# Keys' and values' weights and the context as pairs of float16 in a fused attention and expert kernel

## The chip, the core and the metric

The kernel runs on one core of a Trainium2 chip. A core has five engines that run side by side, each through its own list of instructions in order: TensorE (PE, the matmuls; its weight loads are shown as PEld), VectorE (DVE), ScalarE (ACT), GpSimd (POOL) and SyncE (SP, which here only starts DMA transfers). An engine waits for another by a counter, a semaphore. The metric is the device time of one execution in microseconds (us), lower is better.

## The reference

Eight batches of 512 tokens with 256 channels go through a gated cross attention on a context of 512 rows with 128 channels, and then through eight experts of which each token takes two:

```python
x = x + tanh(g_xattn) * (softmax((LN(x) @ Wq) @ (ctx @ Wk).T / 8) @ (ctx @ Wv) @ Wo + bo)   # 16 heads of 64
probs = softmax(LN(x) @ gate_w.T); comb = the two largest of probs, per token
x = x + tanh(g_ffn) * sum_e comb[e] * (LN(x) @ expert_w[e].T + expert_b[e])
```

All data are float32. The products are made from high and low parts, so that they are nearly as exact as float32: an operand is rounded to a short type (the high part), the remainder is kept as a second one (the low part), and three matmuls, high with high, high with low and low with high, add up in one PSUM bank.

## The kernel before

**Jobs.** A batch is cut into 32 units: 8 pairs of heads times 4 tiles of 128 queries. Per unit PE makes the scores of two heads (`scores`, six matmuls into the bank pair `ST`), DVE takes the row maximum (`nmax`) and the `shifts` from it, ACT the exponential (`exp`, into `pf`) and then its float16 high part (`copy`, into `p_s`), POOL the low part (`low`), SP transposes both by DMA into `pt_s`, and six units later PE multiplies them with the values (`values`, into `PV`). Between units PE makes the other products, called jobs, into three shared banks `MB`: `q`, `k`, `v` (queries, keys, values), `xt`, `ot`, `x2t` (transposes), `wo`, `router`, `pair`, `gates`, `bias` and `bound`. ACT takes a job's high part (`take_hi`), DVE its low part or its sum (`take`); then the bank is free.

**Order.** What each engine does in which of the 32 rows is written out by hand in the tables PE_ORDER, ACT_ORDER, DVE_ORDER and POOL_ORDER, one for the first batch (FIRST), one for the next six (LOOP) and one for the last (LAST). Ahead of FIRST stands a prologue with the jobs `xt0, xt1, bound, k0, q0` of NEXT_JOBS (in LOOP these are jobs for the next batch); behind LAST stand the experts of the last batch (EPI). FIRST also prepares the output's and the experts' weights, which no other batch does.

**What the change touches.** A `k` job is three matmuls of 128x512 of `wk_s` and `kv_s` (L1364), a `v` job three of `kv_s` and `wv_s` (L1368). These three tiles have the type float32r, a float32 form that PE takes in one pass. The high parts are plain copies on ACT (L730, L764, L769; L779 in the loop), the low parts plain subtractions on POOL (L671, L686, L688, L691). `wk` and `wv` land in `pt_s`, which is not used yet, so that SP holds back the second transpose until the low parts are made (L575).

**The bound.** Every batch the row maxima of the context (`kmax`) are multiplied with those of the weights (`kv_w_max`) by PE in the job `bound`. DVE makes of it `v_div`, `v_mul`, `o_mul` and `s_val` (L918 to L973), POOL the scales `k_mul` and `q_out` (`scales`), with which the high and low parts of `k`, `q` and `v` are scaled into float16. In FIRST the job stands in row 21 of PE's table, and DVE takes it in row 22. ACT makes the next batch's context high part (`context`) in row 20, after the exponential of unit 20 and before that of unit 21; in LOOP `bound` stands in row 12 and `context` in row 24.

**Weights of the queries.** `wq` is already handled as a scaled float16 pair: DVE finds the largest weight (`wq_max`), PE sums it over the partitions (`summed`), DVE makes `q_mul` from it, and ACT and DVE make the two parts, the first 256 columns (`early`) in the prologue and the `rest` in FIRST.

Of the kernel before, what the change touches and what calls it, by code (L numbers as in the profile page):

```python
# [218 lines left out]
NEXT_JOBS = [("xt", 0), ("xt", 1), ("bound",), ("k", 0), ("q", 0), ("q", 1), ("k", 1)]  # L219
# [115 lines left out]
def build(nc, x, kv_t, g_xattn, g_ffn, wq, wk, wv, wo, bo, gate_t, expert_t, expert_b, out):  # L335
# [5 lines left out]
    with ctx:  # L341
# [14 lines left out]
        wk_s = sb("wk_s", [P, 2, INNER], F32R)  # L356
        wv_s = sb("wv_s", [P, 2, INNER], F32R)
# [13 lines left out]
        ones = sb("ones", [P, 1])  # L371
        kv_w_max = sb("kv_w_max", [P, 2])
# [17 lines left out]
        kv_s = sb("kv_s", [P, 2, TOKENS], F32R)  # L390
# [47 lines left out]
        stage_q = sb("stage_q", [P, LC, INNER])  # L438
        stage_o = sb("stage_o", [P, PAIRS, DIM])
# [18 lines left out]
        w_hi, wq_lo, wq_rest_lo, w_lo = sem("w_hi"), sem("wq_lo"), sem("wq_rest_lo"), sem("w_lo")  # L458
        late_step, late_hi, late_lo = sem("late_step"), sem("late_hi"), sem("late_lo")
# [52 lines left out]
        CONST_POOL = EXPERTS + 11  # L512
# [17 lines left out]
        def _(sp):  # L530
# [5 lines left out]
            sp.dma_start(stage_k, wk).then_inc(wk_in, 16)  # L536
            sp.dma_start(stage_v, wv).then_inc(wv_in, 16)
# [65 lines left out]
        def _(pool):  # L603
# [81 lines left out]
            pool.wait_ge(kv_hi, 1)  # L685
            pool.tensor_tensor(kv_s[:, 1, :], kvin[:, :], kv_s[:, 0, :].bitcast(F32), ALU.subtract).then_inc(kv_lo, 1)  # L686
            pool.wait_ge(w_hi, 1)
            pool.tensor_tensor(wk_s[:, 1, :], stage_k, wk_s[:, 0, :].bitcast(F32), ALU.subtract).then_inc(w_lo, 1)  # L688
            scales(0)
            pool.wait_ge(w_hi, 3)  # L690
            pool.tensor_tensor(wv_s[:, 1, :], stage_v, wv_s[:, 0, :].bitcast(F32), ALU.subtract).then_inc(w_lo, 1)  # L691
# [6 lines left out]
            def row(it, n):  # L698
                for part in POOL_ORDER[it.kind][n].split():
# [7 lines left out]
                    elif part == "hold3" and it.kind != FIRST:  # L707
                        pool.wait_ge(comb_ready, it.b)
                    elif part == "residual":
                        residual(it)  # L710
                    elif part == "power2" and it.kind != FIRST:
                        power(it.b, ln2_var, ln2_rstd, ln2_shift)
                    elif part == "power1" and it.kind != LAST:
                        power(it.b + 2, ln1_var, ln1_rstd, ln1_shift)
                    elif part == "norm2" and it.kind != FIRST:
                        second_norm(it)
                    elif part == "norm1" and it.kind != LAST:
                        first_norm(it)
# [9 lines left out]
        def _(act):  # L728
            act.wait_ge(kv_in, 16)
            act.activation(kv_s[:, 0, :], kvin[:, :], ACT.Copy).then_inc(kv_hi, 1)  # L730
# [29 lines left out]
            for name in [job for job in JOBS[PRO][:PRO_JOBS] if job in HI[PRO]]:  # L760
                take_hi(pro, name)
                if name == ("xt", LC - 1):
                    act.wait_ge(wk_in, 16)
                    act.activation(wk_s[:, 0, :], stage_k, ACT.Copy).then_inc(w_hi, 1)  # L764
# [3 lines left out]
                    act.wait_ge(wv_in, 16)  # L768
                    act.activation(wv_s[:, 0, :], stage_v, ACT.Copy).then_inc(w_hi, 1)  # L769
                if name == ("q", 0):  # L770
                    act.activation(wq_s[:, 0, :, rest], stage_q[:, :, rest], ACT.Copy, scale=q_mul[:, 0:1])\
                       .then_inc(w_hi, 1)
# [3 lines left out]
            def context_high(it):  # L776
                act.wait_ge(kv_in, 16 * it.b + 32)
                act.wait_ge(job_ready, it.last_done(JOBS, ("k", PAIRS - 1), ("v", TT - 1, 1)))
                act.activation(kv_s[:, 0, :], kvin[:, :], ACT.Copy).then_inc(kv_hi, 1)  # L779
# [74 lines left out]
        def _(dve):  # L854
# [43 lines left out]
            def take(it, name):  # L898
# [18 lines left out]
                elif kind == "bound":  # L917
                    last = dve.tensor_scalar(v_div[:, :], m[:, 0:2], 1.0 / V_RANGE, 1e-30, ALU.mult, ALU.max)  # L918
# [156 lines left out]
            def first_jobs():  # L1075
# [3 lines left out]
                query_scale()  # L1079
                weight_maxima()  # L1080
                take(pro, ("xt", 1))
                early_queries()
                for name in JOBS[PRO][2:PRO_JOBS]:
                    take(pro, name)

            def rest_of_queries():
                dve.wait_ge(w_hi, 4)
# [199 lines left out]
        def _(pe):  # L1287
# [21 lines left out]
            def produce(it, name):  # L1309
# [17 lines left out]
                elif kind == "q" and it.kind == FIRST and name not in NEXT_JOBS:  # L1327
                    pe.wait_ge(wq_rest_lo, 1)
                elif kind == "v" and it.kind == FIRST:
# [40 lines left out]
                elif kind == "bound":  # L1370
                    last = pe.matmul(m[:, 0:2], kmax[:, :].broadcast_to([P, P]), kv_w_max[:, :], start=True, stop=True)
# [99 lines left out]
            def summed(dst, largest, done):  # L1471
                pe.matmul(dst, ones[:, :].broadcast_to([P, P]), largest, start=True, stop=True).then_inc(done, 1)
# [8 lines left out]
            for name in JOBS[PRO][:PRO_JOBS]:  # L1481
# [101 lines left out]
```

## Time and profile before

| | us |
|---|---|
| three runs | 952.51, 953.10, 953.34 (median 953.1) |
| the profiled execution | 954.97 |
| its span from first to last instruction | 952.8 |
| PE, DVE, ACT, POOL busy | 918.6, 853.9, 745.0, 641.6 |
| FIRST, from its first row maximum to that of the next batch | 106.25 |
| the six LOOP batches | 110.93, 111.17, 112.17, 111.41, 111.18, 111.18 |
| LAST, to the end of its last row maximum | 96.06 |
| the rest, EPI | 60.45 |

A stage is measured from one batch's first row maximum on DVE (`nmax`) to the next one's. The busy time of an engine is the time in which at least one of its instructions ran. Matmuls overlap: one of 128x512 float16 lasts 0.38 us by itself, while in a stream one starts every 0.22 us. A row of the views of time below gives the start in us from the span's start, the duration, the engine, the line and the tiles, and in brackets how long the engine had been idle and what ended it.

### The profile page before, as it was taken

To read this page: it belongs to the slowest core of one execution; us is meant where nothing else is said; L and a number is where in the kernel's file an instruction comes from. 1 tells how busy PE (TensorE), PEld (TensorE's weight loads), DVE (VectorE), ACT (ScalarE), POOL (GpSimd) and SP (SyncE) were. 2 spreads that over 40 slices of the span, in tenths; PEclk is the share of its full clock that TensorE was granted. 3 is DMA by queue.
4 is the path that set the end of the run, shared out by engine and by line. 5 is a ranking of instruction groups with operands and counts; after the bars stand their busy time and mean duration, and the time that the engine had idled before them with its cause. 6 is when DMAs were issued, how large, how long until landed. Compare 5 with 4: busy or idle time off the path is not lost.

```text
span 952.8 us, 28718 instructions
## 1 busy us (share of the span) xinstructions
PE 918.6 (96%) x11332; PEld 640.0 (67%) x11332; DVE 853.9 (90%) x1818; ACT 745.0 (78%) x1092; POOL 641.6 (67%) x439
## 2 busy tenths in 40 slices
PE   6788899999999999999999999999999999999997
PEld 4355556777667766777667776677667776667873
DVE  6899999998899989998999988998899988998758
ACT  3899899678995889768896789958898688978510
POOL 4667778586785868577685867858586776866400
PEclk9999999999999999999999999999999999999999
DMA  7599999899997989989999999989899799999800
GB/s 272 105 185 169 167 170 171 163 151 157 192 181 135 158 151 187 178 142 161 167 180 162 153 152 186 180 144 162 146 197 179 133 164 170 163 159 169 130 23 23
DMA packets 549141, 150.97 MB, mean 158 GB/s; under 512 B 537592, under 2 KB 547216, under 8 KB 548752
## 3 DMA queue, kind: packets, MB, share of 16 engines
q1 hardware_dynamic: 549008, 149.13, 92.8%
q8 instruction: 91, 1.49, 0.7%
q14 instruction: 42, 0.34, 0.1%
HBM read 11.70 MB, written 4.19 MB: 17 GB/s over the span
## 4 chain that ended last, share of the span: by engine, by line
PE 77%; DVE 15%; issue 3%; POOL 2%; ACT 1%; DMA 1%; SPq 0%; DVEq 0%; ACTq 0%; POOLq 0%
PE MB L1294 38%; PE PV L1465 16%; PE ST L1443 16%; PE MB L1306 4%; DVE nmax L1001 4%; DVE acc L942 2%; POOL p_s L656 1%; DVE ex_s L1169 1%; PE MB L1379 1%; DMA pt_s<-p_s 1%; PE MB L1384 1%; DVE o_n L1024 1%; DVE QL L981 1%; DVE v_s L992 1%; ACT pf L822 1%
## 5 line engine op out<-in xcount | busy, mean ns | idle before, releaser
L656 POOL TENSOR_TENSOR p_s<-pf,p_s 128x1024 f16<-128x1024 f32 x254 | 543.1, 2140 | 226.7 <-ACT p_s L832 178.5
L822 ACT ACTIVATE pf<-ST,shifts 128x512 f32<-128x512 f32 x512 | 324.0, 690 | 89.8 <-DVE shifts L1007 88.9
L1001 DVE TENSOR_REDUCE nmax<-ST 128x2 f32<-128x1024 f32 x256 | 310.6, 1217 | 15.9 <-PE ST L1443 14.8
L832 ACT ACTIVATE p_s<-pf 128x1024 f16<-128x1024 f32 x254 | 269.3, 1063 | 3.2
L1465 PEld LDWEIGHTS PV<-v_s,pt_s 128*128 128x128 f16 x6096 | 201.2, 97 | 43.1 <-issue 34.9
L1465 PE MATMUL PV<-v_s,pt_s 128*128 128x65 f16 x6096 | 215.5, 193 | 3.5 <-DVE o_n L1024 2.7
L1294 PE MATMUL MB<-ex_s,x2t_s 128*128 128x256 f16 (+1 forms) x1380 | 166.1, 275 | 0.1
L1294 PEld LDWEIGHTS MB<-ex_s,x2t_s 128*128 128x128 f16 x1380 | 131.9, 98 | 21.7 <-issue 1.3
L1443 PE MATMUL ST<-KH,QH 64*128 64x512 f16 x512 | 99.7, 386 | 8.7 <-ACT pf L822 6.9
L961 DVE SCALAR_TENSOR_TENSOR acc<-MB,m,acc 128x256 f32<-128x256 f32 x224 | 95.6, 476 | 4.4 <-PE MB L1294 3.6
L1294 PE MATMUL MB<-xt_s,wq_s 128*128 128x512 f16 x384 | 94.8, 383 | 3.3 <-DVE v_s L992 1.5
L1443 PE MATMUL ST<-KH,QL 64*128 64x512 f16 x512 | 97.9, 379 | 0.0
L1443 PE MATMUL ST<-KL,QH 64*128 64x512 f16 x512 | 97.6, 377 | 0.0
L1294 PE MATMUL MB<-wo_s,ot_s 128*128 128x256 f16 x744 | 91.1, 273 | 0.1
L1294 PEld LDWEIGHTS MB<-wo_s,ot_s 128*128 128x128 f16 x744 | 70.5, 98 | 16.2 <-issue 3.7
L1443 PEld LDWEIGHTS ST<-KH,QH 64*128 64x128 f16 x512 | 24.9, 93 | 63.8 <-issue 29.4
L1294 PEld LDWEIGHTS MB<-xt_s,wq_s 128*128 128x128 f16 x384 | 33.6, 98 | 44.5 <-issue 12.6
L1294 PE MATMUL MB<-wv_s,kv_s 128*128 128x512 f32 x192 | 60.6, 433 | 2.5 <-DVE QL L981 1.9
L1294 PE MATMUL MB<-kv_s,wk_s 128*128 128x512 f32 x192 | 61.8, 431 | 0.6 <-DVE xt_s L984 0.6
L1024 DVE TENSOR_TENSOR o_n<-PV,rden 128x256 f32<-128x256 f32 x127 | 53.9, 425 | 5.4 <-DVE rden L1021 1.2
L981 DVE SCALAR_TENSOR_TENSOR QL<-MB,q_out,QH 128x512 f16<-128x512 f32 x64 | 47.5, 743 | 12.0 <-ACT QH L739 12.0
L743 ACT ACTIVATE KH<-MB,k_mul 128x512 f16<-128x512 f32 x64 | 44.6, 697 | 15.3 <-PE MB L1294 11.8
(160 smaller groups left out, 1025.6 us busy)
## 6 DMA issues: line engine op xcount, KB each, us to landing
pt_s<-p_s SPq DMA_TRANSPOSE x508, 3.4
xin<-x SPq DMA_DIRECT2D x7, 512.0 KB, 4.3
out<-acc SPq DMA_DIRECT2D x7, 512.0 KB, 3.7
kvin<-kv_t SPq DMA_DIRECT2D x8, 256.0 KB, 4.5
stage_e<-expert_t SPq DMA_DIRECT2D x1, 2048.0 KB, 13.3
stage_o<-wo SPq DMA_DIRECT2D x1, 1024.0 KB, 8.8
stage_q<-wq SPq DMA_DIRECT2D x1, 768.0 KB, 6.6
xin<-x SPq DMA_DIRECT2D x2, 256.0 KB, 2.9
```

Of the source, the lines that this page charges most:

```text
L656: pool.tensor_tensor(p_s[:, slot, 1, :, :], pf[:, it.ring(p, u, PF_SLOTS), :, :], p_s[:, slot, 0, :, :], ALU.subtract).then_inc(p_lo, 1)
L743: last = act.activation(KH[:, it.pair_slot(name), :], m[:, :], ACT.Copy, scale=k_mul[:, of % 2:of % 2 + 1])
L822: last = act.activation(pf[:, (n - 1) % PF_SLOTS, i, :], ST[u % 2][:, i, :], ACT.Exp, bias=shifts[:, u % 2, i:i + 1])
L832: act.activation(p_s[:, it.ring(p, u, P_SLOTS), 0, :, :], pf[:, it.ring(p, u, PF_SLOTS), :, :], ACT.Copy).then_inc(p_hi, 1)
L961: last = dve.scalar_tensor_tensor(acc[:, t, :], m[:, DIM * i:DIM * (i + 1)], comb[:, t, e:e + 1], acc[:, t, :], ALU.mult, ALU.add)
L981: last = dve.scalar_tensor_tensor(l_s[:, slot_, :], m[:, :], scale, h_s[:, slot_, :], ALU.mult, ALU.subtract)
L1001: dve.tensor_reduce(nmax[:, t % 2, :, 0], ST[t % 2][:, :, :], AX.X, ALU.max, negate=True)\
L1024: dve.tensor_tensor(dst, outs[:, :, 0:HEAD], rden[:, :].unsqueeze(2).broadcast_to([P, TT, HEAD]), ALU.mult).then_inc(o_ready, 1)
L1294: last = pe.matmul(dst, s, m, start=(k == 0), stop=(k == n - 1))
L1306: last = pe.transpose(bank_[:, tile(t)], src(t), ident[:, :])
L1443: last = pe.matmul(ST[t % 2][:, i, :], queries[r, s, tile(t)], keys[r, s, :], start=(n == 0), stop=(n == len(terms) - 1))
L1465: last = pe.matmul(dst, pt_s[:, slot, a, i, k, :], v_s[:, c, k, (2 * p + i) % HEADS, :], start=(k == 0 and n == 0), stop=(k == TT - 1 and ...
```

## The change

The keys' and values' weights and the context become scaled float16 pairs like the queries' weights. Each gets a scale from its largest value (`w_div` and `w_mul` for the weights, `c_div` and `c_mul` for the context). The context's scale comes, in the prologue, from a product of its own, and in later batches from a third column in the bound's product; `v_mul` takes both scales in. ACT's high parts are scaled copies; on POOL a low part is now two operations, a scaling in place and a subtraction. `wk` and `wv` have staging tiles of their own (SP's hold is gone). In the prologue only the first 256 columns of `wk` are prepared; the other 768 and all of `wv` follow, and the queries' product `q0` goes ahead of the keys' `k0`. The tables of order are the same.

```diff
-NEXT_JOBS = [("xt", 0), ("xt", 1), ("bound",), ("k", 0), ("q", 0), ("q", 1), ("k", 1)]
+NEXT_JOBS = [("xt", 0), ("xt", 1), ("bound",), ("q", 0), ("k", 0), ("q", 1), ("k", 1)]
-        wk_s = sb("wk_s", [P, 2, INNER], F32R)
-        wv_s = sb("wv_s", [P, 2, INNER], F32R)
+        wk_s = sb("wk_s", [P, 2, INNER], F16)
+        wv_s = sb("wv_s", [P, 2, INNER], F16)
-        kv_s = sb("kv_s", [P, 2, TOKENS], F32R)
+        kv_s = sb("kv_s", [P, 2, TOKENS], F16)
...
+            def context_low(of):
+                pool.wait_ge(kv_hi, of + 1)
+                pool.wait_ge(kv_scale, of + 1)
+                pool.tensor_scalar(kvin[:, :], kvin[:, :], c_mul[:, 0:1], 1.0, ALU.mult, ALU.mult).then_inc(kv_scaled, 1)
+                pool.wait_ge(kv_scaled, of + 1)
+                pool.tensor_tensor(kv_s[:, 1, :], kvin[:, :], kv_s[:, 0, :], ALU.subtract).then_inc(kv_lo, 1)
+            def weight_low(n, w, raw, cols, of):
+                pool.wait_ge(w_hi, 4 + n)
+                pool.tensor_scalar(raw[:, cols], raw[:, cols], w_mul[:, of:of + 1], 1.0, ALU.mult, ALU.mult)\
+                    .then_inc(w_scaled, 1)
+                pool.wait_ge(w_scaled, n + 1)
+                pool.tensor_tensor(w[:, 1, cols], raw[:, cols], w[:, 0, cols], ALU.subtract).then_inc(w_lo, 1)
...
             def context_high(it):
+                act.wait_ge(kv_scale, it.b + 2)
+                act.activation(kv_s[:, 0, :], kvin[:, :], ACT.Copy, scale=c_mul[:, 0:1]).then_inc(kv_hi, 1)
...
                     elif part == "ph":
+                        act.activation(wv_s[:, 0, :], stage_v[:, :], ACT.Copy, scale=w_mul[:, 0:1]).then_inc(w_hi, 1)
                         for name in DEFERRED:
                             take_hi(pro, name)
...
                 elif kind == "bound":
+                    if it.kind != PRO:
+                        dve.tensor_scalar(c_div[:, :], m[:, 2:3], 1.0 / W_RANGE, 1e-30, ALU.mult, ALU.max)
                     last = dve.tensor_scalar(v_div[:, :], m[:, 0:2], 1.0 / V_RANGE, 1e-30, ALU.mult, ALU.max)
...
-                        dve.reciprocal(v_mul[:, of % 2, :], v_div[:, :])
+                        if of:
+                            dve.reciprocal(c_mul[:, :], c_div[:, :]).then_inc(kv_scale, 1)
+                        dve.reciprocal(v_rec[:, :], v_div[:, :]).then_inc(v_step, 1)
+                        dve.wait_ge(v_step, of + 1)
+                        dve.scalar_tensor_tensor(v_mul[:, of % 2, :], w_div[:, :], c_div[:, 0:1], v_rec[:, :],
+                                                 ALU.mult, ALU.mult)
...
-                    last = pe.matmul(m[:, 0:2], kmax[:, :].broadcast_to([P, P]), kv_w_max[:, :], start=True, stop=True)
+                    last = pe.matmul(m[:, 0:3], kmax[:, :].broadcast_to([P, P]), kv_w_max[:, :], start=True, stop=True)
```

POOL's list from the end of the prologue to the first low parts of FIRST, before:

```order
L686 TENSOR_TENSOR kv_s<-kvin,kv_s 128x512
L688 TENSOR_TENSOR wk_s<-pt_s,wk_s 128x1024
L662 TENSOR_TENSOR root<-s_val,half 128x1
L664 TENSOR_TENSOR k_mul<-v_mul,root 128x1
L666 TENSOR_SCALAR q_out<-root 128x1
L691 TENSOR_TENSOR wv_s<-pt_s,wv_s 128x1024
L680 TENSOR_TENSOR x<-xin,bo_t 128x1024
L656 TENSOR_TENSOR p_s<-pf,p_s 128x1024 x15
```

The same place of POOL's list now:

```order
L679 TENSOR_SCALAR kvin<-kvin,c_mul 128x512
L681 TENSOR_TENSOR kv_s<-kvin,kv_s 128x512
L668 TENSOR_TENSOR root<-s_val,half 128x1
L670 TENSOR_TENSOR k_mul<-v_mul,root 128x1
L672 TENSOR_SCALAR q_out<-root 128x1
L686 TENSOR_SCALAR stage_k<-stage_k,w_mul 128x768
L689 TENSOR_TENSOR wk_s<-stage_k,wk_s 128x768
L686 TENSOR_SCALAR stage_v<-stage_v,w_mul 128x1024
L689 TENSOR_TENSOR wv_s<-stage_v,wv_s 128x1024
L697 TENSOR_TENSOR x<-xin,bo_t 128x1024
L662 TENSOR_TENSOR p_s<-pf,p_s 128x1024 x15
```

The weights' low parts went behind the scales and each became a scaling and a subtraction; the residual `x` and the low parts of the probabilities stand behind them.

ACT's list from the prologue's last jobs into FIRST, before (`pf` is the exponential, x4 those of units 0 and 1):

```order
L743 ACTIVATE KH<-MB,k_mul 128x512
L739 ACTIVATE QH<-MB,q_out 128x512
L771 ACTIVATE wq_s<-stage_q,q_mul 128x2x768
L774 ACTIVATE tg<-gates 128x2
L822 ACTIVATE pf<-ST,shifts 128x512 x4
L739 ACTIVATE QH<-MB,q_out 128x512
L743 ACTIVATE KH<-MB,k_mul 128x512
```

And now:

```order
L751 ACTIVATE QH<-MB,q_out 128x512
L755 ACTIVATE KH<-MB,k_mul 128x512
L785 ACTIVATE wq_s<-stage_q,q_mul 128x2x768
L787 ACTIVATE wk_s<-stage_k,w_mul 128x768
L790 ACTIVATE tg<-gates 128x2
L840 ACTIVATE pf<-ST,shifts 128x512 x4
L814 ACTIVATE wv_s<-stage_v,w_mul 128x1024
L751 ACTIVATE QH<-MB,q_out 128x512
L755 ACTIVATE KH<-MB,k_mul 128x512
```

The high part of `wv` went from the prologue to the place behind the exponential of unit 1.

DVE's list around the bound in a LOOP batch, before (`rden`, `o_n` normalise an output, `xn` is the router's result):

```order
L1024 TENSOR_TENSOR o_n<-PV,rden 128x256
L918 TENSOR_SCALAR v_div<-MB 128x2
L970 RECIPROCAL v_mul<-v_div 128x2
L1040 TENSOR_TENSOR o_mul<-v_div,o_back 128x1
L973 TENSOR_TENSOR s_val<-v_div,q_back 128x1
L920 TENSOR_SCALAR xn<-MB,g_back 16x512
```

And now:

```order
L1049 TENSOR_TENSOR o_n<-PV,rden 128x256
L937 TENSOR_SCALAR c_div<-MB 128x1
L938 TENSOR_SCALAR v_div<-MB 128x2
L991 RECIPROCAL c_mul<-c_div 128x1
L992 RECIPROCAL v_rec<-v_div 128x2
L994 SCALAR_TENSOR_TENSOR v_mul<-w_div,c_div,v_rec 128x2
L1065 TENSOR_TENSOR o_mul<-v_div,o_back 128x1
L998 TENSOR_TENSOR s_val<-v_div,q_back 128x1
L940 TENSOR_SCALAR xn<-MB,g_back 16x512
```

Three small operations came in between `o_n` and `o_mul`, one of them behind a wait for its forerunner.

## Rows read from the trace of the kernel before

**Rows 1.** Busy time by stage, FIRST, one LOOP batch and LAST: stretch, length, engines

```profile
22.00:128.25 106.25, 88.06 (x1035) 51.79 (x1031) 101.19 (x177) 96.30 (x145) 75.65 (x44) 0.97 0.94 154
239.18:350.35 111.17, 111.17 (x1416) 78.84 (x1414) 101.59 (x220) 91.69 (x135) 80.12 (x54) 1.00 0.98 165
796.29:892.35 96.06, 95.98 (x1275) 66.58 (x1272) 88.02 (x182) 84.47 (x124) 72.11 (x41) 1.00 1.05 168
```

**Rows 2.** The same, instructions on tile kv_s alone (PE, PEld, ACT, POOL)

```profile
239.18:350.35 111.17, 15.13 (x48) 7.95 (x48) 0.64 (x1) 1.27 (x1) 1.00 0.98 165
796.29:892.35 96.06, 12.80 (x42) 6.99 (x42) 0.00 (x0) 0.00 (x0) 1.00 1.05 168
```

**Rows 3.** The same, instructions on tile wq_s alone (PE, PEld, DVE, ACT)

```profile
239.18:350.35 111.17, 11.70 (x48) 4.17 (x48) 0.00 (x0) 0.00 (x0) 1.00 0.98 165
```

**Rows 4.** Groups by line and form: count, busy us, mean ns of one

```profile
L656 POOL TENSOR_TENSOR p_s<-pf,p_s 128x1024 f16<-128x1024 f32 x254 | 543.1, 2140 | 226.7 <-ACT p_s L832 178.5 <-DVE comb_w L1248 39.3 <-DVE w L1219 4.1
...
L1294 PE MATMUL MB<-xt_s,wq_s 128*128 128x512 f16 x384 | 94.8, 383 | 3.3 <-DVE v_s L992 1.5 <-DVE ot_s L989 1.3 <-DVE wq_s L1088 0.6
...
L637 POOL TENSOR_SCALAR xn<-xin,rstd,shift 128x256 f32<-128x256 f32 x28 | 15.7, 572 | 0.0
...
L769 ACT ACTIVATE wv_s<-pt_s 128x1024 fp32r<-128x1024 f32 x1 | 1.0, 1041 | 0.0
```

**Rows 5.** Instructions in order of time on PE, 424.3 to 429.3 us

```profile
424.41 1.47 PE L1294 MATMUL MB<-ex_s,x2t_s 128*128 128x256 f16 x12
425.64 0.95 PE L1294 MATMUL MB<-kv_s,wk_s 128*128 128x512 f32 x3
426.42 0.39 PE L1391 MATMUL MB<-eb_s,gates_t 72*128 72x256 f32 x2
...
428.25 0.96 PE L1294 MATMUL MB<-kv_s,wk_s 128*128 128x512 f32 x3
429.06 0.42 PE L1465 MATMUL PV<-v_s,pt_s 128*128 128x65 f16 x8
```

**Rows 6.** Instructions in order of time, all engines, 0 to 45 us

```profile
21.13 0.39 PE L1443 MATMUL ST<-KH,QH 64*128 64x512 f16 x2 [1.57 <-DVE QL L981]
...
26.57 1.27 ACT L822 ACTIVATE pf<-ST,shifts 128x512 f32<-128x512 f32 x2 [1.78 <-DVE shifts L1007]
...
29.35 2.68 PE L1294 MATMUL MB<-wv_s,kv_s 128*128 128x512 f32 x6 [1.86 <-DVE QL L981]
...
33.32 1.23 DVE L1001 TENSOR_REDUCE nmax<-ST 128x2 f32<-128x1024 f32 x1 [1.35 <-PE ST L1443]
```

**Rows 7.** Busy time in one stretch: PE, PEld, DVE, ACT, POOL, granted clock

```profile
29.60:33.00 3.40, 3.40 (x12) 1.62 (x11) 2.37 (x5) 2.55 (x5) 2.73 (x2) 0.50 0.40 77
```

**Rows 8.** Instructions in order of time around FIRST's bound, 86 to 100 us

```profile
90.81 0.63 ACT L779 ACTIVATE kv_s<-kvin 128x512 fp32r<-128x512 f32 x1
...
92.89 1.27 ACT L822 ACTIVATE pf<-ST,shifts 128x512 f32<-128x512 f32 x2
...
93.72 2.13 POOL L656 TENSOR_TENSOR p_s<-pf,p_s 128x1024 f16<-128x1024 f32 x1
...
94.02 0.14 DVE L918 TENSOR_SCALAR v_div<-MB 128x2 f32<-128x2 f32 x1
...
94.28 1.58 DVE L1040 TENSOR_TENSOR o_mul<-v_div,o_back 128x1 f32<-128x1 f32 x1
...
96.69 1.21 DVE L1001 TENSOR_REDUCE nmax<-ST 128x2 f32<-128x1024 f32 x1
```

**Rows 9.** The same around the bound of a LOOP batch, 275 to 281 us

```profile
278.09 0.15 DVE L918 TENSOR_SCALAR v_div<-MB 128x2 f32<-128x2 f32 x1
...
278.41 0.15 DVE L973 TENSOR_TENSOR s_val<-v_div,q_back 128x1 f32<-128x1 f32 x1
...
278.76 2.13 POOL L656 TENSOR_TENSOR p_s<-pf,p_s 128x1024 f16<-128x1024 f32 x1 [0.69 <-ACT p_s L832]
...
280.09 1.05 PE L1384 MATMUL MB<-fold,xn 16*128 16x8 f32 x8
```

More of the change, by code:

```diff
@@ L370, in build @@
         zero = sb("zero", [P, TT])
-        ones = sb("ones", [P, 1])
-        kv_w_max = sb("kv_w_max", [P, 2])
+        ones = sb("ones", [P, 2])
+        kv_w_max = sb("kv_w_max", [P, 3])
+        w_div = sb("w_div", [P, 2])
+        w_mul = sb("w_mul", [P, 2])
+        c_div = sb("c_div", [P, 1])
+        c_mul = sb("c_mul", [P, 1])
+        v_rec = sb("v_rec", [P, 2])
         wq_max = sb("wq_max", [P, 2])
@@ L684, in _ @@
             power(1, ln1_var, ln1_rstd, ln1_shift)
[L685 to L688, printed above, removed]
+            context_low(0)
             scales(0)
-            pool.wait_ge(w_hi, 3)
-            pool.tensor_tensor(wv_s[:, 1, :], stage_v, wv_s[:, 0, :].bitcast(F32), ALU.subtract).then_inc(w_lo, 1)
+            weight_low(0, wk_s, stage_k, rest, 1)
+            weight_low(1, wv_s, stage_v, slice(0, INNER), 0)
             count = {}
@@ L767, in _ @@
                        .then_inc(w_hi, 1)
[L768 to L770 removed]
+                    act.wait_ge(kv_in, 16)
+                    act.wait_ge(kv_scale, 1)
+                    act.activation(kv_s[:, 0, :], kvin[:, :], ACT.Copy, scale=c_mul[:, 0:1]).then_inc(kv_hi, 1)
+                    act.wait_ge(w_scale, 1)
+                    act.activation(wk_s[:, 0, early], stage_k[:, early], ACT.Copy, scale=w_mul[:, 1:2])\
+                       .then_inc(w_hi, 1)
+                if name == ("k", 0):
                     act.activation(wq_s[:, 0, :, rest], stage_q[:, :, rest], ACT.Copy, scale=q_mul[:, 0:1])\
+                       .then_inc(w_hi, 1)
+                    act.activation(wk_s[:, 0, rest], stage_k[:, rest], ACT.Copy, scale=w_mul[:, 1:2])\
                        .then_inc(w_hi, 1)
@@ L778, in context_high @@
                 act.wait_ge(job_ready, it.last_done(JOBS, ("k", PAIRS - 1), ("v", TT - 1, 1)))
-                act.activation(kv_s[:, 0, :], kvin[:, :], ACT.Copy).then_inc(kv_hi, 1)
+                act.wait_ge(kv_scale, it.b + 2)
+                act.activation(kv_s[:, 0, :], kvin[:, :], ACT.Copy, scale=c_mul[:, 0:1]).then_inc(kv_hi, 1)
             count = {}
@@ L1079, in first_jobs @@
                 query_scale()
+                context_scale()
                 weight_maxima()
                 take(pro, ("xt", 1))
+                weight_scales()
                 early_queries()
-                for name in JOBS[PRO][2:PRO_JOBS]:
-                    take(pro, name)
+                take(pro, ("bound",))
+                early_keys()
+                take(pro, ("q", 0))
+                take(pro, ("k", 0))
             def rest_of_queries():
-                dve.wait_ge(w_hi, 4)
+                dve.wait_ge(w_hi, 3)
                 dve.scalar_tensor_tensor(wq_s[:, 1, :, rest], stage_q[:, :, rest], q_mul[:, 0:1],
@@ L1328, in produce @@
                     pe.wait_ge(wq_rest_lo, 1)
+                elif kind == "k" and it.kind == FIRST and name not in NEXT_JOBS:
+                    pe.wait_ge(w_lo, 1)
                 elif kind == "v" and it.kind == FIRST:
@@ L1471, in summed @@
             def summed(dst, largest, done):
-                pe.matmul(dst, ones[:, :].broadcast_to([P, P]), largest, start=True, stop=True).then_inc(done, 1)
+                pe.matmul(dst, ones[:, 0:1].broadcast_to([P, P]), largest, start=True, stop=True).then_inc(done, 1)
             def keep_busy(n):
@@ L1487, in _ @@
                     pe.wait_ge(kv_lo, 1)
-                    pe.wait_ge(w_lo, 1)
+                    pe.wait_ge(wk_lo, 1)
+                if name == ("bound",):
+                    pe.wait_ge(kv_largest, 1)
+                    summed(sums_w, kv_w_max[:, 0:2], kv_w_summed)
                 produce(pro, name)
+                if name == ("xt", 0):
+                    pe.wait_ge(kmax_step, 1)
+                    pe.matmul(sums_c, kmax[:, :].broadcast_to([P, P]), ones[:, :], start=True, stop=True)\
+                      .then_inc(kv_summed, 1)
                 if name == ("xt", LC - 1):
```

49 lines of the change are left out of this document (28 added, 21 removed).

## The prediction

> **What bounds the kernel now.** I read the busy time stage by stage first, then the groups of instructions by form, then PE's list in order of time, and last the prologue and FIRST's bound in order of time. In a LOOP batch PE is busy in 111.17 of 111.17 us, and in LAST in 95.98 of 96.06, while DVE has 101.59 and 88.02 [rows 1]; there a shorter PE instruction can shorten the stage. In FIRST it is the other way round: DVE is busy in 101.19 of 106.25 us and PE in 88.06, so PE's saving buys nothing there, and whatever makes DVE wait is paid. The reader is to see in these rows that one edit has two prices. A change to the weights' types touches PE in seven batches, and its preparations touch the prologue and FIRST only.
>
> **The gain on PE.** In one LOOP batch the 48 matmuls on `kv_s` (keys and values, float32r) keep PE busy for 15.13 us [rows 2]. The 48 on `wq_s` are of the same form in float16 and take 11.70 [rows 3]. These come as eight jobs of six, the others as sixteen jobs of three, and each job ends with one matmul that runs out by itself. One float16 matmul lasts 0.383 us [rows 4]; a job of six takes 11.70/8 = 1.46, so the step from one start to the next is (1.46 - 0.383)/5 = 0.216 us, and a tail is 0.383 - 0.216 = 0.17. With sixteen tails in place of eight the float16 form of the keys and values would be busy for 11.70 + 8 x 0.17 = 13.06. The difference, 15.13 - 13.06 = 2.07 us per batch, is the upper end.
>
> What counts is how much earlier the next job starts. Behind scores a float32 job starts at 428.25 and the next matmul at 429.06, 0.81 us for three, against 3 x 0.216 = 0.65: 0.16 saved. Behind another product, as at 425.64, the job's first start overlaps the work before it, which runs from 424.41 to 425.88, and from there to the next product at 426.42 there is 0.54, less than three float16 steps: I take 0.05 saved there [rows 5]. Eleven of the sixteen jobs are of the first sort by PE's list: 11 x 0.15 + 5 x 0.05 = 1.9 us per batch. LAST has 42 of 48 such matmuls [rows 2], so 1.6. That makes 6 x 1.9 + 1.6 = 13.0. Where PE follows the exponential closely a little of it becomes idle time; I take 12.0, with 13.5 as the upper bound (2.07 throughout, less some waiting) and 6 as the lower one, if half of the jobs stand in front of a wait.
>
> **The prologue and FIRST's first rows.** Before, the first scores start at 21.13, the exponential of unit 1 runs from 26.57 to 27.84, the first `v` jobs start at 29.35 (released by DVE's low queries, so their weights were there), and the row maximum that waits for the scores behind them at 33.32 [rows 6]. Now ACT makes `wv`'s high part only behind that exponential: 1.04 us [rows 4] to 28.9. POOL then scales 128x1024, an operation that the trace doesn't have. The nearest row is the scaling of 128x256 in 0.572 us [rows 4]; four of those are 2.29, and the lower bound is one, 0.6. I take 1.7, nearer the upper, since the elements are four times as many. Then comes the subtraction of 128x1024. POOL's one of that size takes 2.14 [rows 4], so it ends at about 32.7 and `v` starts some 3.5 us later than at 29.35. PE is behind it in order, so the next scores and the maximum at 33.32 move by as much. Shorter products give nothing back there: the granted clock is 0.50 from 29.6 to 33.0 [rows 7]. The residual and the first low parts queue on POOL behind the same two operations. Bounds: 2.5 (a scaling at its lower bound) to 4.5 (the preceding scaling and subtraction of `wk`'s rest still in the way); taken 3.5.
>
> The first scores move too. On DVE's way to them stand the scales of the context and of the weights, `v_rec`, the product that makes `v_mul`, and the early keys: five small operations and one of 128x256. Small ones that hang on each other start every 0.10 to 0.15 us, as `v_div` to `s_val` in a LOOP bound shows [rows 9]; seven such steps are 0.7 to 1.1. POOL's context low part gets a scaling of 128x512 (two of 0.572, 1.14) ahead of its subtraction, and `k0` stands behind `q0`. On the other hand ACT no longer makes the whole of `wk` and `wv` ahead of `q0` and `k0`, twice about 1.04. Bounds -0.8 to +1.4; taken +0.8, what DVE's steps add.
>
> **FIRST's bound.** ACT's `context` stands in row 20 and ran at 90.81; the exponential of unit 21 is behind it, at 92.89. DVE takes the bound in row 22, at 94.02 [rows 8]. The change makes `context` wait for `c_mul`, which DVE makes out of that bound: at about 94.02 + 3 x 0.15 = 94.5. Behind the waiting instruction on ACT stand a copy, a job's high part and the exponential of unit 21, whose end frees the bank for the scores of unit 23; for these waits DVE's maximum. From `context` to the exponential it was 92.89 - 90.81 = 2.08, so it starts at 96.6 and ends at 97.9; with the scores (about 1.0, six starts of at most 0.22 us) the maximum comes at 98.9 instead of 96.69: +2.2. It is a loop across three engines that passes only because DVE still has work ahead of the bound. DVE's `o_mul` there took 1.58 us beside POOL's low part at 93.72 [rows 8]; that low part now comes later, and this stall goes away, which is within the bounds of 1 to 3.
>
> **What is hidden.** In LOOP the bound stands in row 12 and `context` in row 24, so its wait costs nothing. DVE's three more operations there add about 0.35 us per batch on an engine with 9.6 us to spare. The fold of the logits starts on PE at 280.09 and `s_val` ends at 278.56 [rows 9]; with 0.35 and the sum that follows there is still about 0.7 us over. POOL gets 1.14 us more per context, on an engine busy for 80.12 of 111.17 us [rows 1]. The bound's third column, one more memset and SP's lost hold I cost at nothing: the first is one column of a product that takes one instruction either way, the memset lies beside the first loads, and the hold was passed, since the low parts were there before the second transpose came up. If that cover were gone the hold would be a small gain.
>
> **The sum.** -12.0 + 3.5 + 0.8 + 2.2 and 0.2 for ACT's and POOL's longer lists in FIRST: -5.3 us. Against the profiled execution's own 954.97 that is 949.7; this execution lies 1.9 above the median of the runs shown, 953.1, so the forecast is 947.8.
>
> **Rivals.** (A) PE's saving is given back inside LOOP: DVE has 101.59 us of work, the exponential waits for its shifts, and the order is a fixed list, so each unit may wait for a maximum, not for PE. Against it: PE shows no idle time at all in the batch. With 6 of the 12 gone, the lower bound of the gain, and the costs as above the sum is +0.7, about 953.8.
>
> (B) The other side. In LOOP POOL's low part starts at 278.76, 0.67 us after `v_div` starts at 278.09; `s_val` starts before it, at 278.41 [rows 9]. With three more operations and one wait in front, `s_val` comes at `v_div` + 0.66. If POOL starts first, DVE's small operations stand until it is done, as FIRST's `o_mul` did, from 94.28 to 95.86 with POOL busy from 93.72 to 95.85 [rows 8]. Then `s_val` comes some 2 us later, past the slack at 280.09, and PE, with everything behind the logits in order, waits about 1.7 us, in six batches 10. The sum becomes +5, about 958: slower. The decision point is 0.67 us between `v_div` and the last of the small operations. For it speaks how near 0.66 is; against it that POOL's start waits for ACT's `p_s` and may move too, and that a stalled `s_val` need not be the logits' last wait.
>
> The Trainium skill's page "SBUF — State Buffer", section "Who interferes with whom", says that a VectorE instruction with two SBUF inputs and a GpSimd one that reads SBUF share a port, and that whoever comes first holds it for its whole instruction while the other stands. The trace agrees with that in the 1.58 us of `o_mul`. By that rule the new product for `v_mul` would stand as well.
>
> (C) The costs in the prologue and FIRST are hidden by DVE's other work, and only the gain shows: 947.8 - 6.7 = 941.1 if all of them are, and about 943 if two of the 6.7 stay. For it speaks that DVE in FIRST has work that doesn't hang on the scores; against it that it is busy in 95% of the stage, so that work pushed back isn't regained.
>
> (D) The change doesn't do what it says: float16 jobs with three matmuls take as long as float32 ones from start to start. Then only the costs are left, +6.7, about 960. Against it stand the 0.81 and the 0.65 above.
>
> **How the numbers follow.** Forecast 0.55; A 0.17; B 0.12; C 0.10; D 0.06. The range runs from 943, the edge of C, to 957, which takes in A and part of B; D and the far half of B are left out. The forecast's own range is 944 to 951.2: the gain 1.5 more or 2 less, each cost about 1 off, not all on one side. A difference under 0.2%, 1.9 us, can't be told from no change; by the cases faster has 0.64 (the forecast but for its upper edge, and C), no change 0.17 (A, mostly), slower 0.19 (B, D and a little of A).
>
> **What would show it.** In the profile after: PE's busy time on `kv_s` in a LOOP batch at about 13.1 us, the batch at about 109.3; the first `v` job's start about 4 us later, released by POOL; FIRST longer by about 6; in FIRST ACT's `kv_s` at about 94.5, released by DVE, and the exponential behind it. In LOOP `s_val` before POOL's low part. The prediction is wrong if LOOP keeps its 111 us, if PE waits at the logits' fold, or if FIRST's length hardly moves.

## The result and the profile after

The changed kernel takes 977.21 us (median of 4 runs, 974.66 to 979.43) against 952.81 before: a ratio of 1.0256 (95% interval 1.0229 to 1.0283). It is slower by 24.4 us, where a time 5.3 us shorter was forecast. The profiled execution has a span of 972.9 us against 952.8.

Busy time by stage after: FIRST, the first three LOOP batches, LAST and EPI. Behind the stretch stand its length, the busy times of PE, PEld, DVE, ACT and POOL, the granted clock, the DMA share and GB/s; they answer to [rows 1].

```profile
22.44:133.97 111.53, 86.00 (x1035) 46.81 (x1031) 101.25 (x180) 97.88 (x148) 83.67 (x49) 0.97 0.78 157
133.97:245.93 111.96, 109.66 (x1414) 74.92 (x1412) 103.43 (x224) 91.36 (x135) 80.61 (x55) 1.00 0.89 163
245.93:361.04 115.11, 112.99 (x1416) 77.07 (x1414) 103.57 (x224) 91.28 (x135) 80.59 (x55) 0.97 0.89 159
361.04:474.62 113.58, 111.46 (x1416) 76.04 (x1414) 103.54 (x223) 91.33 (x135) 80.57 (x55) 0.98 0.83 161
...
818.40:913.57 95.17, 94.73 (x1275) 63.31 (x1272) 87.77 (x182) 84.26 (x124) 72.02 (x41) 1.00 0.98 171
913.57:972.80 59.23, 51.49 (x476) 36.45 (x473) 40.87 (x103) 6.00 (x10) 2.05 (x5) 0.99 0.15 39
```

A LOOP batch has become longer, not shorter. It has about 2 us in which PE is idle, and the six batches of one execution come in three lengths (111.96, 113.57 or 113.58, 115.10 or 115.11 us), in step with the granted clock (1.00, 0.98, 0.97). The reason stands in the waits of PE over the whole span (line, who is waited for, us in total, times, the longest):

```profile
PE MB L1435 <- DVE xn L940: 11.1, 6, 1.9
PE ST L1494 <- ACT pf L840: 10.2, 10, 3.6
PE MB L1343 <- POOL wv_s L689: 4.9, 1, 4.9
```

The first line is new: six times, once per LOOP batch, the fold of the logits (eight small matmuls on the router's result `xn`) waits 1.9 us. In order of time around the bound of the first LOOP batch, as [rows 9]:

```profile
172.49 0.15 DVE L937 TENSOR_SCALAR c_div<-MB 128x1 f32<-128x1 f32 x1
...
172.55 0.15 DVE L938 TENSOR_SCALAR v_div<-MB 128x2 f32<-128x2 f32 x1
...
173.00 2.15 DVE L994 SCALAR_TENSOR_TENSOR v_mul<-w_div,c_div,v_rec 128x2 f32<-128x2 f32 x1
173.01 2.12 POOL L662 TENSOR_TENSOR p_s<-pf,p_s 128x1024 f16<-128x1024 f32 x1 [0.69 <-ACT p_s L850]
...
175.14 0.15 DVE L998 TENSOR_TENSOR s_val<-v_div,q_back 128x1 f32<-128x1 f32 x1
175.32 0.74 DVE L940 TENSOR_SCALAR xn<-MB,g_back 16x512 f32<-16x512 f32 x1
...
176.21 1.02 PE L1435 MATMUL MB<-fold,xn 16*128 16x8 f32 x8 [1.85 <-DVE xn L940]
```

`v_mul`, 256 numbers, lasts 2.15 us: it ends when POOL's low part ends, and so it does in all six batches. `s_val`, `xn` and the fold are late by that. What follows on PE in the second LOOP batch is seen in stretches of 3 us (columns as above):

```profile
285.00:288.00 3.00, 1.33 (x9) 0.68 (x7) 2.96 (x5) 3.00 (x5) 2.54 (x2) 1.00 1.11 308
288.00:291.00 3.00, 2.82 (x33) 2.82 (x34) 2.87 (x7) 1.33 (x3) 1.68 (x1) 0.59 1.28 250
291.00:294.00 3.00, 3.00 (x32) 1.71 (x31) 0.60 (x2) 0.21 (x1) 0.00 (x0) 0.50 1.22 119
294.00:297.00 3.00, 3.00 (x18) 1.08 (x15) 1.81 (x2) 1.54 (x3) 1.50 (x1) 0.78 0.45 102
```

Behind the stretch with 1.33 us of PE work the granted clock is at its lower level, 1.2 GHz, until about 295. In the first LOOP batch it stayed at 1.00, and there the batch is 111.96 long.

The steps foreseen for the prologue and FIRST are there as well. The values' weights ahead of the first `v` job, as [rows 6], and FIRST's bound, as [rows 8]:

```profile
28.16 1.14 ACT L814 ACTIVATE wv_s<-stage_v,w_mul 128x1024 f16<-128x1024 f32 x1
...
29.41 1.12 POOL L686 TENSOR_SCALAR stage_v<-stage_v,w_mul 128x1024 f32<-128x1024 f32 x1 [2.26 <-ACT wv_s L814]
...
30.61 2.13 POOL L689 TENSOR_TENSOR wv_s<-stage_v,wv_s 128x1024 f16<-128x1024 f32 x1
...
32.80 1.03 PE L1343 MATMUL MB<-wv_s,kv_s 128*128 128x512 f16 x2 [4.86 <-POOL wv_s L689]
```

```profile
97.50 0.16 DVE L991 RECIPROCAL c_mul<-c_div 128x1 f32<-128x1 f32 x1
...
97.78 0.72 ACT L796 ACTIVATE kv_s<-kvin,c_mul 128x512 f16<-128x512 f32 x1 [3.62 <-DVE c_mul L991]
...
99.96 1.24 ACT L840 ACTIVATE pf<-ST,shifts 128x512 f32<-128x512 f32 x2
...
101.26 0.61 PE L1494 MATMUL ST<-KH,QH 64*128 64x512 f16 x2 [3.61 <-ACT pf L840]
...
102.76 1.23 DVE L1026 TENSOR_REDUCE nmax<-ST 128x2 f32<-128x1024 f32 x1 [3.80 <-PE ST L1494]
```

### The profile page after: what moved, and what is told of

Read it like the earlier page. It is cut to its first block, busy times and chain, and to the rows that moved or that the text cites. A ratio compares the mean times of both kernels' runs of the same rounds, so it can differ in the third digit from the quotient of the medians.

```text
span 972.9 us, 28780 instructions
## 1 busy us (share of the span) xinstructions
PE 918.1 (94%) x11336; PEld 616.0 (63%) x11336; DVE 865.2 (89%) x1845; ACT 743.4 (76%) x1093; POOL 648.1 (67%) x450
## 4 chain that ended last, share of the span: by engine, by line
PE 58%; DVE 26%; ACT 8%; issue 7%; DMA 1%; POOL 0%; SPq 0%; ACTq 0%; DVEq 0%
PE MB L1343 30%; PE PV L1516 11%; PE ST L1494 11%; DVE nmax L1026 9%; ACT p_s L850 3%; ACT pf L840 3%; PE MB L1355 3%; DVE v_s L1017 2%; DVE QL L1006 2%; DVE o_n L1049 2%; DVE KL L1006 1%; PE ST L1343 1%; DVE stats L884 1%; PE MB L1435 1%; DVE shifts L1032 1%
## 5 line engine op out<-in xcount | busy, mean ns | idle before, releaser
L1026 DVE TENSOR_REDUCE nmax<-ST 128x2 f32<-128x1024 f32 x256 | 310.0, 1215 | 25.9 <-PE ST L1494 24.4
L1516 PEld LDWEIGHTS PV<-v_s,pt_s 128*128 128x128 f16 x6096 | 208.9, 99 | 41.8 <-issue 24.8
L1516 PE MATMUL PV<-v_s,pt_s 128*128 128x65 f16 x6096 | 220.3, 195 | 3.1 <-DVE o_n L1049 3.0
L1343 PE MATMUL MB<-wv_s,kv_s 128*128 128x512 f16 x192 | 53.0, 389 | 6.2 <-POOL wv_s L689 4.9
L1343 PE MATMUL MB<-kv_s,wk_s 128*128 128x512 f16 x192 | 55.2, 399 | 1.3 <-DVE KL L1006 1.3
```

The costliest lines, as they stand in the source:

```text
L1026: dve.tensor_reduce(nmax[:, t % 2, :, 0], ST[t % 2][:, :, :], AX.X, ALU.max, negate=True)\
L1343: last = pe.matmul(dst, s, m, start=(k == 0), stop=(k == n - 1))
L1516: last = pe.matmul(dst, pt_s[:, slot, a, i, k, :], v_s[:, c, k, (2 * p + i) % HEADS, :], start=(k == 0 and n == 0), stop=(k == TT - 1 and ...
```

## The experiments

Theory P: in LOOP a small DVE operation with two tensor inputs stands for as long as POOL's low part runs, and PE's idle time behind it costs clock on top. Its rivals are C (the clock falls because float16 products leave PE less busy) and Q (DVE's list is just longer). The letters in the expectations are these. Ratios are to the kernel before, run beside each.

**One tensor input (e1).** All three operations of the bound that have two:

```diff
-dve.scalar_tensor_tensor(v_mul[:, of % 2, :], w_div[:, :], c_div[:, 0:1], v_rec[:, :], ALU.mult, ALU.mult)
+for n in range(2):
+    dve.tensor_scalar(v_mul[:, of % 2, n:n + 1], v_rec[:, n:n + 1], w_div[:, n:n + 1], c_div[:, 0:1], ALU.mult, ALU.mult)
...
-dve.tensor_tensor(s_val[:, :], v_div[:, 1:2], q_back[:, :], ALU.mult).then_inc(scale_done, 1)
+dve.tensor_scalar(s_val[:, :], v_div[:, 1:2], q_back[:, 0:1], None, ALU.mult).then_inc(scale_done, 1)
...
-dve.tensor_tensor(o_mul[:, b % 2:b % 2 + 1], v_div[:, 0:1], o_back[:, :], ALU.mult)
+dve.tensor_scalar(o_mul[:, b % 2:b % 2 + 1], v_div[:, 0:1], o_back[:, 0:1], None, ALU.mult)
```

> v_mul, o_mul and s_val are made by TENSOR_SCALAR with one tensor input each (the other factors as per-partition scalars; v_mul in two instructions). Theory P (a DVE operation with two tensor inputs stands behind POOL's low part, and the clock falls behind PE's idle 1.85 us): v_mul about 0.15 us, no gap before the logits' fold, granted clock 1.00 in LOOP, a LOOP batch of 109.5 to 111, the whole 948 to 954. Rival C (the clock falls by itself, since float16 products leave PE less busy): the gap goes, but batches at 0.97 stay, about 966. Rival Q (DVE's longer list and its own wait make the bound late, not the port): still 1.85 us idle per batch, about 977.

956.44 us, ratio 1.0028 (1.0018 to 1.0037): some 21 of the 24 us come back. The LOOP batches are as P says, while the whole lies 2.4 us above the range expected for it. In order of time at the second LOOP batch's bound, and that batch as a whole:

```profile
287.56 0.45 DVE L995 TENSOR_SCALAR v_mul<-v_rec,w_div,c_div 128x1 f32<-128x1 f32 x2
287.57 2.13 POOL L662 TENSOR_TENSOR p_s<-pf,p_s 128x1024 f16<-128x1024 f32 x1 [0.69 <-ACT p_s L850]
...
288.05 0.20 DVE L999 TENSOR_SCALAR s_val<-v_div,q_back 128x1 f32<-128x1 f32 x1
...
289.17 1.02 PE L1436 MATMUL MB<-fold,xn 16*128 16x8 f32 x8 [0.26 <-DVE xn L940]
```

```profile
248.50:358.90 110.40, 109.87 (x1416) 75.03 (x1414) 101.91 (x225) 91.22 (x135) 80.57 (x55) 1.00 0.90 166
```

DVE runs four operations beside POOL without standing, although there is one more of them. Float16 products with a gap of only 0.26 us ahead of the fold have a clock of 1.00 in all six batches. Q and C fall. The Trainium skill, "SBUF — State Buffer", section "Who interferes with whom", says that a VectorE instruction with at most one SBUF input, outside the two-port modes, does not contend with GpSimd. These rows agree, if factors that are read as per-partition scalars are not counted as inputs.

**`v_mul` alone (e1b):** the first two changed lines above, nothing else.

> Only v_mul is made by TENSOR_SCALAR (two instructions); o_mul and s_val keep two tensor inputs. P: they come some 0.6 us after v_div, POOL's low part starts 0.46 after it, so they stand instead, about 2 us, and the time stays at 972 to 978. If the three-operand form of v_mul is what stands, not two inputs as such: as with one input everywhere, 948 to 954.

972.74 us, ratio 1.0216 (1.019 to 1.0243). Now the next two-input operation stands:

```profile
174.31 2.13 POOL L662 TENSOR_TENSOR p_s<-pf,p_s 128x1024 f16<-128x1024 f32 x1 [0.69 <-ACT p_s L850]
...
174.67 1.77 DVE L1066 TENSOR_TENSOR o_mul<-v_div,o_back 128x1 f32<-128x1 f32 x1
```

So it is neither `v_mul` nor its three-operand form, but whichever two-input operation is not through before POOL starts. Behind the gap, here 1.79 us, the clock fell in four of the six batches.

**The steps alone, float32r kept (e2).** In the kernel before, with `w_div` and `c_div` set to ones:

```diff
+if it.kind != PRO:
+    dve.tensor_scalar(d_div[:, :], m[:, 0:1], 1.0 / V_RANGE, 1e-30, ALU.mult, ALU.max)
...
-dve.reciprocal(v_mul[:, of % 2, :], v_div[:, :])
+if of:
+    dve.reciprocal(c_mul[:, :], d_div[:, :])
+dve.reciprocal(v_rec[:, :], v_div[:, :]).then_inc(v_step, 1)
+dve.wait_ge(v_step, of + 1)
+dve.scalar_tensor_tensor(v_mul[:, of % 2, :], w_div[:, :], c_div[:, 0:1], v_rec[:, :], ALU.mult, ALU.mult)
```

> The kernel before, float32r products and all, with DVE's three more small steps in the bound alone (v_mul by the two-input form with constants of one, and two idle ones). P: v_mul or its neighbours stand for up to 2.1 us behind POOL, PE idles about 1.8 us per LOOP batch, the clock falls behind it: 965 to 980. C: PE idles, but float32r products hold the clock: about 963 at most, clock 1.00. Q without a port: three small steps, 953 to 955.

971.89 us, ratio 1.0199 (1.0174 to 1.0225). These few small DVE instructions alone bring most of the loss. `s_val` is the one that is caught, `o_mul` is just through:

```profile
282.51 0.15 DVE L1055 TENSOR_TENSOR o_mul<-v_div,o_back 128x1 f32<-128x1 f32 x1
282.53 2.14 POOL L662 TENSOR_TENSOR p_s<-pf,p_s 128x1024 f16<-128x1024 f32 x1 [0.69 <-ACT p_s L838]
...
282.58 2.11 DVE L988 TENSOR_TENSOR s_val<-v_div,q_back 128x1 f32<-128x1 f32 x1
```

Its LOOP batches are 114.15 to 115.91 long at a clock of 0.97 to 0.99, with float32r products, and the clock fell in all six; that too speaks against C. The second of them:

```profile
243.03:358.92 115.89, 114.21 (x1416) 81.10 (x1414) 103.86 (x223) 91.62 (x135) 80.00 (x54) 0.97 0.86 158
```

**Filling PE's gap (e3, e3b).** In e3 eight products of 128x512 stand ahead of the fold, into the fold's own bank:

> The changed kernel with eight more float16 matmuls of 128x512 on PE in front of the wait of the logits' fold, LOOP only, into the bank that the fold writes next; the stall of v_mul stays. P: the gap of 1.85 us is filled with work, the clock stays 1.00, batches of about 112, 962 to 967. C: the clock falls all the same, 974 to 980.

978.24 us, ratio 1.0253 (1.0237 to 1.0269), a miss of the experiment: that bank is the router's, so the fillers waited for DVE too and ran behind the gap, which stayed at 1.86. Still the clock was 1.00 in all six batches (113.84 to 113.86 each): with dense products right behind an idle 1.86 us it stayed up, where it had not with the small products of the fold. The second LOOP batch:

```profile
252.56:366.41 113.85, 111.70 (x1424) 75.70 (x1422) 103.67 (x224) 91.41 (x135) 80.64 (x55) 1.00 0.89 160
```

In e3b sixteen of 128x228 write into unused columns of `PV` and run inside the gap:

> The changed kernel (the stall of v_mul kept) with sixteen float16 matmuls of 128x228 on PE ahead of the wait of the logits' fold in LOOP, into columns of PV that nothing uses: this time they run inside the idle 1.85 us, not behind it. P with the clock as a consequence of the idle time: the clock stays 1.00 in LOOP, a batch 112.0, the whole 964 to 968 (977.2 less the 12 to 13 us of half clock). If the stall itself and not the idle PE goes with the loss: batches of 113 to 115 stay, 975 to 979.

963.56 us, ratio 1.0104 (1.009 to 1.0118), 0.4 under what P was expected to give. `v_mul` still stands for 2.16 us, and the clock is 1.00 in all six batches. The second LOOP batch:

```profile
248.45:360.43 111.98, 111.42 (x1432) 76.58 (x1430) 103.45 (x224) 91.32 (x135) 80.56 (x55) 1.00 0.90 163
```

The stall itself therefore costs 111.98 - 110.40 = 1.6 us per batch, 9.4 over the six, and the half clock behind it 12.6 in the profiled execution (684.4 us for six batches against 671.8 here). The changed kernel's own first LOOP batch, with the stall and a clock of 1.00, is 111.96 long as well.

**What float16 is worth (e4):** e1 with the three tiles as float32r again.

```diff
-        wk_s = sb("wk_s", [P, 2, INNER], F16)
-        wv_s = sb("wv_s", [P, 2, INNER], F16)
+        wk_s = sb("wk_s", [P, 2, INNER], F32R)
+        wv_s = sb("wv_s", [P, 2, INNER], F32R)
...
-        kv_s = sb("kv_s", [P, 2, TOKENS], F16)
+        kv_s = sb("kv_s", [P, 2, TOKENS], F32R)
...
```

> As e1_one_input, but the weights of keys and values and the context are float32r again, with all scales, order and preparations kept: what float16 alone is worth. By the forecast's own term (12.0 us) the time is e1's ratio plus 12 us, ratio about 1.015, LOOP batches above 112. By the rows of e1 (a LOOP batch 0.77 shorter than before, LAST 0.9) plus what DVE's longer list costs: 4.5 to 8 us over e1, ratio 1.0075 to 1.011, LOOP batches of 111.1 to 111.7, LAST 96.1.

959.75 us, ratio 1.0071 (1.0059 to 1.0083). Three of its stages, LOOP, LOOP and LAST:

```profile
246.99:358.21 111.22, 111.16 (x1416) 78.85 (x1414) 102.15 (x225) 91.66 (x135) 80.78 (x55) 1.00 0.88 165
358.21:469.40 111.19, 111.14 (x1416) 78.86 (x1414) 102.12 (x224) 91.64 (x135) 80.74 (x55) 1.00 0.88 165
...
803.00:899.03 96.03, 95.95 (x1275) 66.57 (x1272) 87.95 (x182) 84.39 (x124) 72.08 (x41) 1.00 0.95 169
```

Float16 gives 4.5 us in the six LOOP batches (666.96 us here, 662.43 in e1), about 0.8 each, and 0.9 in LAST: 5.4 in sum, where 12.0 were forecast. The whole differs by 4.1 us by the ratios, just under the 4.5 to 8 expected from the rows of e1, and by 3.3 in the profiles, where FIRST can't be compared: it ran at a granted clock of 0.94 here and of 0.91 in e1. Two single runs of equal mean clock, 0.990, took 959.38 us in e4 and 953.88 in e1, 5.5 apart.

**FIRST's two costs (e5, e6, e7).** On top of e1: in e5 `wv` goes ahead of the rest of `wk`, on ACT ahead of the first exponential and on POOL; in e6 `context` moves in FIRST of ACT_ORDER; e7 has both.

```diff
-weight_low(0, wk_s, stage_k, rest, 1)
-weight_low(1, wv_s, stage_v, slice(0, INNER), 0)
+weight_low(0, wv_s, stage_v, slice(0, INNER), 0)
+weight_low(1, wk_s, stage_k, rest, 1)
...
-"exp context copy lh", "exp lh hi copy", "exp hi hi copy", "exp lh copy lg",
+"exp copy lh", "exp lh hi copy", "exp hi hi copy", "exp lh copy context lg",
```

> As e1_one_input, with the values' weights ahead of the rest of the keys' on ACT (ahead of the first exponential) and on POOL: the first v job no longer waits 4.9 us for POOL. If the forecast's term is right (+3.5 in the first rows), FIRST gets 2.5 to 3.5 shorter, ratio 0.9990 to 1.0005. Rival (DVE's backlog in FIRST takes it up): FIRST within 0.8 of e1's, ratio 1.0028.

952.39 us, ratio 0.9987 (0.9976 to 0.9998): 3.9 us under e1 by the ratios. FIRST is 108.88 long, 2.7 less than in the changed kernel:

```profile
22.97:131.85 108.88, 87.24 (x1035) 47.17 (x1031) 100.69 (x181) 97.89 (x148) 83.82 (x49) 0.95 0.79 158
```

> As e1_one_input, with the context's high part in FIRST moved on ACT from row 20 to row 23, behind DVE's bound. If the forecast's term is right (+2.2), the gap of 3.6 us before the scores of unit 23 goes and FIRST gets 1.5 to 3 shorter, ratio 0.9995 to 1.0012. Rival: the wait moves on to the keys of the next batch (k1), or DVE's work fills it, ratio 1.0028.

950.2 us, ratio 0.9969 (0.9958 to 0.998): 5.6 us under e1 by the ratios, more than twice the forecast's term and more than was expected here. FIRST is 4.8 shorter than in the changed kernel:

```profile
22.89:129.67 106.78, 84.51 (x1035) 46.51 (x1031) 100.02 (x181) 97.94 (x148) 84.19 (x49) 0.98 0.84 163
```

> e1, e5 and e6 together. If the costs add up: 4 to 6 us below e1, 950 to 952, ratio 0.9965 to 0.9985, faster than before by the net gain of LOOP and LAST. Rival (what is taken from one wait is given to the next): not below 953, ratio 1.000 or more.

946.01 us, ratio 0.9925 (0.9913 to 0.9937), 9.8 us under e1, about the sum of both (9.5) and more than the 4 to 6 expected, and 7.1 us faster than before: the best version. FIRST and a LOOP batch of e7:

```profile
23.11:126.53 103.42, 84.43 (x1035) 46.56 (x1031) 98.91 (x181) 97.72 (x148) 84.03 (x49) 0.98 0.89 168
...
236.90:347.30 110.40, 109.86 (x1416) 75.00 (x1414) 101.88 (x224) 91.30 (x135) 80.62 (x55) 1.00 0.90 166
```

Part of these gains is the clock: FIRST ran at 0.91 in e1's profile and at 0.95, 0.98 and 0.98 in those of e5, e6 and e7. Runs of one mean clock, 0.991, took 953.77 us in e1, 952.46 in e5, 950.18 in e6 and 946.78 and 946.89 in e7, that is 1.3, 3.6 and 7.0 less; but for e7's two they are single runs, so this is rough.

**The place of `context` alone (e8):** the second hunk above, in the kernel before.

> The kernel before with one thing moved: FIRST's context on ACT from row 20 to row 23. It shows how much of the gain of e6 and e7 over the kernel before is owed to the place alone. If context's place was harmless before (it did not wait): FIRST within 1 us of 106.25, ratio 0.999 to 1.001. If any copy ahead of the exponential of unit 21 costs its own length there: FIRST 1 to 3 us shorter, ratio 0.997 to 0.999.

953.91 us, ratio 0.9997 (0.9989 to 1.0006), FIRST 106.25: the place cost nothing while `context` waited for nothing.

**After what LOOP gave back (e9):** e7 with two units of values ahead of `k5`.

```diff
-"scores k5 values values x2t0 ot0",
+"scores values values k5 x2t0 ot0",
```

> e7_both with one move on PE in LOOP: two units of values ahead of job k5, which waited 0.28 us for its bank (DVE's low part of k3). If the part of PE's saving that LOOP gave back sits in such waits: batches of 110.1 to 110.2, 1 to 2 us below e7, ratio 0.9905 to 0.992. Rival (the wait moves to the next job, as before): batches of 110.4 stay, ratio 0.9925.

957.09 us, ratio 1.0036 (1.0022 to 1.005), a miss: batches of 112.1. PE's waits in one of them:

```profile
PE ST L1495 <- ACT pf L840: 1.2, 1, 1.2
PE PV L1517 <- DVE o_n L1050: 0.9, 1, 0.9
PE MB L1436 <- DVE xn L940: 0.2, 1, 0.2
```

The wait for a bank ahead of `k5`, 0.2 us, is gone; in its place stand 2.1 us of waiting for an output to be normalised and for an exponential.

## Why the prediction was wrong, point by point

**What failed** is the step "DVE's three more operations there add about 0.35 us per batch on an engine with 9.6 us to spare", put under "What is hidden", that is at nothing. What the runs showed in its place is a stall of 1.6 us per batch and a half clock behind it, 22.0 us together in the profiled execution. The rival B named the mechanism and the place and priced the stall well (10 us; it cost 9.4), but had a chance of 0.12. Four things were off.

- The margin was measured to the wrong instruction: not `s_val` at `v_div` + 0.66 decides, but the first two-input operation, which is now `v_mul`, 0.45 behind `v_div`.
- POOL's start was taken as fixed at 0.67 behind `v_div`. With one more operation ahead of `v_div` it is 0.60 (282.53 - 281.93 in e2; the same in e4, which has DVE's list of e1 with float32r), and with float16 products 0.46 (173.01 - 172.55). So the gain itself brought POOL's start 0.14 nearer.
- The slack at the fold was not 0.7. Before, `xn` ended at 279.34, 0.75 ahead of the fold at 280.09, and 0.35 of that was to go, which leaves 0.40.

```profile
278.60 0.74 DVE L920 TENSOR_SCALAR xn<-MB,g_back 16x512 f32<-16x512 f32 x1
```

- Of the price only the stall was seen; the half clock behind it costs 12.6 us more. In the LOOP batch of [rows 1] PE had no idle time and a clock of 1.00, so these rows held no price for a first gap there; FIRST's clock of 0.97 [rows 1], in a stage with gaps, was the hint.

**The gain on PE.** Its working up to the start-to-start step was right: from start to start the 48 matmuls on `kv_s` took 13.29 us in the second LOOP batch before and 11.41 in e1's, 1.9 less, as forecast. What stayed is 0.8. Other steps grew by 1.1 from start to start: 0.40 behind scores, 0.19 each behind the queries' products and the bias, the rest in smaller pieces. Only a part of that is waiting that the profile shows. The waits of e1's second LOOP batch are

```profile
PE MB L1436 <- DVE xn L940: 0.3, 1, 0.3
PE MB L1344 <- DVE KL L1007: 0.2, 1, 0.2
```

where before had none (the first of them is already within the 11.41). That is rival A in small; what the other growth comes from is not shown. The net, 5.4 in LOOP and LAST, is under the lower bound of 6.

**Prologue and FIRST.** First scores later: forecast 0.8, and the first row maximum came 0.45 later (22.44 against 22.00). That is no measure of the term, for it comes at 22.83 in e8, with the old prologue, and at 23.78 in e1, with the new one.

`v` later: forecast 3.5, measured 3.45 (32.80 against 29.35), by two errors that cancel: POOL's scaling took 1.12, not 1.7, and began at 29.41, some 0.5 later than forecast. Counted from the first row maximum `v` is 3.0 later, and e5's FIRST is 2.7 shorter.

`context`: forecast 2.2, by e6 5.6, or 3.6 at an equal clock. The exponential behind it began 6.6 us later in FIRST than before (77.5 against 70.9 from the first maximum). In e5, where `v` is early, it began at 74.8, so 2.7 of the 6.6 are the late `v`, and 3.9 are the wait itself, for which the forecast had 3.7 (96.6 against 92.89). What was priced too low comes behind it. The row maximum after the scores of unit 23 came at 74.7 before, at 77.6 in e5 and at 73.3 in e7, where `context` doesn't wait: with the wait it is 2.9 later than before, and 4.3 later than without it. And the scores of unit 23 in the changed kernel, behind 3.6 us without PE work, ran at half clock, 0.61 us for the first two against 0.39 for such a pair in LOOP:

```profile
101.00:104.00 3.00, 2.74 (x10) 0.81 (x11) 1.24 (x2) 3.00 (x6) 1.33 (x2) 0.50 0.66 147
```

FIRST as a whole came out 5.3 longer against 5.9 forecast, but by two errors: these costs are about 8 (111.53 - 103.42), and without them FIRST is 2.8 shorter than before, which the forecast had ruled out. Part of it may be the `o_mul` of 1.58 us that no longer stands, part PE's 3.6 us less work; no run tells these apart.

**The account** of the 20.0 us by which the stages of the two profiles differ: first maximum +0.4, FIRST +5.3, stall +9.4, half clock +12.6, shorter products and the rest of LOOP -5.6, LAST -0.9, EPI -1.2. EPI's is not the change: e8, with the old code there, has 58.94 too. The medians differ by 24.4, since the other three runs of the changed kernel, 976.5 to 979.4 us, have a mean granted clock of 0.971 to 0.975 against 0.98.

## What to carry to other kernels

Before adding an instruction of a few numbers to an engine "with time to spare", look at what starts on the neighbour engine within half a microsecond of it, and give it one tensor input where the other factor is one number per partition. A gap of PE in a stage that had none is to be priced twice, for itself and for the clock behind it. A new wait on an in-order engine goes behind the work it would hold up: moving `context` cost one word in a table and gave 5.6 us, of which about 2 go with the clock.

## What was not expected of the hardware

Behind an idle 1.85 us of PE followed by the fold's eight small products the clock fell to its lower level in five of six batches (behind 1.79 us in four of six in e1b, behind 1.68 in six of six in e2); behind the same 1.86 us followed by eight products of 128x512 (e3) it fell in none of six. And DVE's `v_mul` stands in the record as started 0.01 us ahead of POOL's operation and stood all the same, while in e2 an `o_mul` 0.02 ahead got through, in all six batches of either: who is first can't be read from starts that close.
